# Moving the identity expert's eight wide operations from VectorE to GpSimd in an RWKV + mixture-of-experts layer

## The reference, cut to what matters

```python
x = x + rwkv(layernorm(x))                     # time-mix attention, not touched here
hid = layernorm(x)
probs = softmax(hid @ router_w + router_bias)  # 16 experts
top_w, top_i = top_k(probs, 2)
combine = one_hot(top_i, 16) * normed(top_w)   # zero for all but two experts of a token
routed = combine[:, 15:16] * hid               # expert 15 is the identity
for e in range(15):
    y = silu(hid @ gate_w[e]) * (hid @ up_w[e]) @ down_w[e]
    routed = routed + combine[:, e:e+1] * y
shared = silu(causal_conv3(hid)) * (hid @ shared_up_w) @ shared_down_w
out = x + shared + routed
```

## Time and profile before

| | us |
|---|---|
| median of 3 runs | 2799.32 (2798.11 to 2801.17) |
| the profiled execution's own time | 2799.06 |
| its span, on the slowest core (core 6) | 2797.3 |
| spans of the eight cores | 2783.8 to 2797.3 |
| busy on core 6: TensorE matmuls | 1857.6 |
| busy on core 6: VectorE | 1234.5 |
| busy on core 6: ScalarE | 364.3 |
| busy on core 6: GpSimd | 67.9 |

### The profile page before, as it was taken

The page is one execution under the profiler, slowest core; times in us unless marked ns, Lnnn a source line. Parts: engine busy times, 40 slices in busy tenths (PEclk is TensorE's granted clock), DMA queues, the critical chain, the costliest instruction groups (busy, mean ns, idle before and its releaser), DMA issues.

```text
span 2797.3 us, 21491 instructions; the slowest of 8 cores (2783.8 to 2797.3 us)
## 1 busy us (share of the span) xinstructions
PE 1857.6 (66%) x7497; PEld 784.3 (28%) x7648; DVE 1234.5 (44%) x1708; ACT 364.3 (13%) x615; POOL 67.9 (2%) x88
## 2 busy tenths in 40 slices
PE   3524336134043698788887887888878878888787
PEld 1201112011011243333333333333333333333333
DVE  4483583662666612344243343442433434434244
ACT  0411420323200000100100001001010010010100
POOL 0000000000010000000000000000000000000000
PEclk8756658577565799899998988989989989889898
DMA  7603305114062100212132132121321311213102
GB/s 151 120 1 60 60 0 90 30 21 70 0 91 45 25 0 1 35 18 38 18 51 38 16 53 34 20 38 16 53 38 16 53 21 32 38 16 53 31 0 120
DMA packets 69306, 112.77 MB, mean 40 GB/s; under 512 B 2592, under 2 KB 37424, under 8 KB 68160
## 3 DMA queue, kind: packets, MB, share of 16 engines
q0 software_dynamic: 63856, 94.50, 22.1%
q1 hardware_dynamic: 5344, 16.91, 1.7%
HBM read 197.28 MB, written 8.52 MB: 74 GB/s over the span
## 4 chain that ended last, share of the span: by engine, by line
PE 53%; DVE 10%; issue 2%; ACT 1%; DVEq 0%; DMA 0%; ACTq 0%; POOLq 0%
PE pc L704 18%; PE pc L730 16%; PE pc L718 15%; DVE h L773 4%; DVE sg L772 4%; PE pc L669 2%; PE pc L688 1%; ACT sg L802 1%; PE pc L677 1%; DVE acc L746 1%; DVE h L743 1%; DVE acc L781 1%; DVE h L755 0%; DVEq L36 0%; DMA cb<-comb_dram 0%
## 5 line engine op out<-in xcount | busy, mean ns | idle before, releaser
L704 PE MATMUL pc<-ln2x,wsl 128*128 128x512 bf16 x1882 | 511.5, 435 | 194.8 <-ACT sg L802 190.5
L730 PE MATMUL pc<-h,wsl 128*128 128x512 bf16 x1882 | 458.8, 404 | 104.4 <-DVE h L773 100.3
L772 DVE TENSOR_TENSOR sg<-sg,pc 128x512 f32<-128x512 f32 x240 | 165.0, 687 | 817.3 <-PE pc L718 798.3
L718 PE MATMUL pc<-ln2x,wsl 128*128 128x512 bf16 x1881 | 425.1, 380 | 2.1
L781 DVE TENSOR_TENSOR acc<-acc,pc 128x512 f32<-128x512 f32 x480 | 330.0, 688 | 184.5 <-PE pc L730 145.0
L704 PEld LDWEIGHTS pc<-ln2x,wsl 128*128 128x128 bf16 x1920 | 205.2, 109 | 500.0 <-issue 336.8
L802 ACT ACTIVATE sg<-pc 128x512 f32<-128x512 f32 x240 | 143.3, 597 | 1519.3 <-PE pc L704 1012.5
L730 PEld LDWEIGHTS pc<-h,wsl 128*128 128x128 bf16 x1920 | 190.2, 102 | 373.1 <-issue 192.8
L718 PEld LDWEIGHTS pc<-ln2x,wsl 128*128 128x128 bf16 x1920 | 187.6, 98 | 230.2
L371 PE MATMUL pb<-mx,wsla 128*128 128x512 bf16 x501 | 128.6, 421 | 180.4 <-DVE mx L225 156.9
L371 PE MATMUL pb<-sry,wsla 128*128 128x512 bf16 x251 | 65.0, 424 | 189.9 <-DVE sry L277 94.9
(11 more groups left out here) (121 smaller groups left out, 913.8 us busy)
## 6 DMA issues: line engine op xcount, KB each, us to landing
wsl<-gw POOLq DMA_DIRECT2D x15, 1024.0 KB, 9.5
wsl<-uw POOLq DMA_DIRECT2D x15, 1024.0 KB, 10.3
wsl<-dw POOLq DMA_DIRECT2D x15, 1024.0 KB, 10.4
acc<-x SPq DMA_DIRECT2D x4, 2048.0 KB, 24.9
wsla<-wk POOLq DMA_DIRECT2D x4, 2048.0 KB, 16.9
wsla<-wv POOLq DMA_DIRECT2D x4, 2048.0 KB, 18.4
wsla<-wr POOLq DMA_DIRECT2D x4, 2048.0 KB, 28.2
wsla<-wo POOLq DMA_DIRECT2D x4, 2048.0 KB, 16.9
```

Source lines behind the costliest of these rows:

```text
L704: inst = t.matmul(pc4[tc][:], slot_ap(3 * e)[:, kc, ocI * 128:(ocI + 1) * 128], ln2x[:, kc, 2 + tc * 512: 2 + (tc + 1) * 512], start=(kc = ...
L718: inst = t.matmul(pc4[4 + tc][:], slot_ap(3 * e + 1)[:, kc, ocI * 128:(ocI + 1) * 128], ln2x[:, kc, 2 + tc * 512: 2 + (tc + 1) * 512], sta ...
L730: inst = t.matmul(pc4[(oc % 2) * 4 + tc][:], slot_ap(3 * e + 2)[:, kcI, oc * 128:(oc + 1) * 128], h[:, kcI, tc * 512:(tc + 1) * 512], star ...
L772: VS.do(lambda sl=sl, tc=tc: v.tensor_tensor(sl[:], sl[:], pc4[4 + tc][:], OP.mult))
```

## The change

The eight operations of the identity expert leave VectorE's list and stand, with the same operands and the same order, at the head of GpSimd's list in `blk4`. GpSimd issues the DMA for row 15, waits for it itself, does the eight operations one behind the other, and only then issues the DMAs for rows 0 and 1; the wait for `v:id3` ahead of row 1 falls away, since GpSimd is now itself the reader of `cb[1]`. VectorE's list in the block begins with a wait for `g:id3`, the last of the eight, ahead of the first `hsh`.

```diff
-                gp_seq = ["comb15", "comb0", "comb1"]
+                gp_seq = ["comb0", "comb1"]
...
                 @blk4.gpsimd
                 def _(g):
+                    GS.eng = g
+                    g.dma_start(fl(cb[1][:]),
+                                comb_d[15][None, :].broadcast_to([128, T])).then_inc(s_cb[1], 16)
+                    g.wait_ge(s_cb[1], 16)
+                    for tc in range(4):
+                        cbc = cb[1][:, tc, :].unsqueeze(1).broadcast_to([128, CC, 512])
+                        hf = fl(h[:]).bitcast(F32).rearrange("p (cc t) -> p cc t", t=512)
+                        GS.do(lambda tc=tc, cbc=cbc, hf=hf: g.tensor_tensor(
+                            hf[:], ln2x[:, :, 2 + tc * 512: 2 + (tc + 1) * 512], cbc, OP.mult))
+                        dst = acc[:, :, tc * 512:(tc + 1) * 512] if "id" in parts else hf[:]
+                        GS.do(lambda tc=tc, dst=dst, hf=hf: g.tensor_tensor(
+                            dst, acc[:, :, tc * 512:(tc + 1) * 512], hf[:], OP.add), f"id{tc}")
...
                             if nm == "comb1":
-                                g.wait_ge(s_dv, MS("v:id3"))
+                                pass
...
                 @blk4.vector
                 def _(v):
                     VS.eng = v
-                    v.wait_ge(s_cb[1], 16)
-                    for tc in range(4):
-                        cbc = cb[1][:, tc, :].unsqueeze(1).broadcast_to([128, CC, 512])
-                        hf = fl(h[:]).bitcast(F32).rearrange("p (cc t) -> p cc t", t=512)
-                        VS.do(lambda tc=tc, cbc=cbc, hf=hf: v.tensor_tensor(
-                            hf[:], ln2x[:, :, 2 + tc * 512: 2 + (tc + 1) * 512], cbc, OP.mult))
-                        dst = acc[:, :, tc * 512:(tc + 1) * 512] if "id" in parts else hf[:]
-                        VS.do(lambda tc=tc, dst=dst, hf=hf: v.tensor_tensor(
-                            dst, acc[:, :, tc * 512:(tc + 1) * 512], hf[:], OP.add), f"id{tc}")
+                    v.wait_ge(s_gp, MS("g:id3"))
```

## The result

The changed kernel takes 2823.94 us (median of 10 runs) beside 2799.19 us of the kernel before on the same chips: the ratio is 1.0087, with a 95% interval of 1.0075 to 1.0099, thus 24.4 us more (21 to 28). The forecast was 2836, that is 37 us more, with 2815 to 2872 as its range.

What follows compares the result with a forecast made beforehand. The identity expert, ending last ahead of the first hsh, was taken to bound the block's start. 8 x 8.85 + 8 x 0.3 - 36.24 = +37.0 us on 2799.06 gave 2836 us, range 2815 to 2872.

Steps and rivals of the forecast that it cites:

- What bounds the place: Start of the feed-forward block: the identity expert ends 12.5 us after the up projection, so any lengthening is paid in full.
- The price of the eight operations: Identity expert on GpSimd: 8.85 us an operation, twice VectorE's 4.425, with ends of 2.29 and 15.5 us.
- The gaps: Between GpSimd's eight operations: 0.3 us each, taken between 0.11 and 0.53, 2.4 us in all.
- TensorE's clock after the longer wait: Ahead of the shared down projection: idle time grows from 15.86 to about 53 us; nothing added, 1.3 us either side.
- Costed at nothing with their cover: DMAs of rows 0 and 1 go out at about 1004; row 0 is first read at 1119.64, so no cost.
- What is after it follows rigidly: Behind the first hsh: four chunks and 15 experts shift with the delay, their length unchanged.
- Three passes: Rival on GpSimd's price: two reads and the write take turns, 13.3 us an operation, 2871 us; chance of 11.0 to 13.3 us 0.14.
- A load at first use: Rival ahead of GpSimd's first tensor operation: a load of 1.3 us, 2837, or about 6 us, 2842; chance 0.10.
- Faster: Rival: GpSimd at the bf16 product's 2.29 us an operation, hsh 12.4 us sooner, 2787 us; chance 0.03.
- no change: Rival: GpSimd at VectorE's own rate, +1.6 us, 2801; holds between 3.5 and 4.9 us an operation; chance 0.03.

Runs made afterwards that it cites:

- probe: The changed kernel with twelve more operations and two memsets on GpSimd while it waits for the first expert; 2825.4 us in one run.
- gp_apart: The changed kernel with a separate scratch tile for GpSimd's product, so no wait ahead of the first hsh; median 2789.9 us, ratio 0.9921.
- pad_ve: The changed kernel with eight memsets of 8 columns on VectorE ahead of its wait for g:id3; 2835.4 us in one run.

## Why the prediction was right, and where its sum was off

- **What bounds the place.** Right, to the tenth of a microsecond. The identity expert ended last and was paid in full: the wait of TensorE ahead of the down projection grew from 15.86 to 45.66 us, and leaving the work out won 12.4 us, the amount that was read from the rows.
- **The price of the eight operations.** The mis-sized term. It was put at 8 x 8.85 = 70.8 us, two passes of VectorE's time each. The additions fit, at 8.81; the products took 7.31, since their two bf16 inputs, one of them broadcast, are cheaper on GpSimd than two f32 ones (in `probe` and `gp_apart`, for 2048 elements: 4.51 us for f32, 4.05 for bf16, 3.75 for bf16 with the broadcast), while VectorE takes 4.425 us for both the earlier trace rows. Measured: 4 x 8.81 + 4 x 7.31 = 64.5 us. Two passes was a choice; `probe` supports it in so far as one input costs about half of two. The figure of the Trainium skill, "GPSIMD Engine Reference", section 3.1, agrees for f32: its 4497 ns for 2048 elements stand beside the 4.51 us of `gp_apart`'s additions. For the bf16 pair that table has no figure, and the prediction's 9.0 us would have been 1.7 us too much.
- **The gaps.** Put at 2.4 us, they were 1.3 us: 0.15 us between two of GpSimd's operations (937.20 to 937.35) and 0.31 us from the last to `hsh`. The 0.53 us of the row used as upper bound was the way to a DMA, not to an operation.
- **So far the sum** would have been 64.46 + 1.32 - 36.24 = +29.5 us instead of +37.0.
- **TensorE's clock after the longer wait.** Nothing added, within 1.3 us; right: the first down projection took 8.55 us after 45.66 us of idle time, beside 9.79 before, so the threefold idle time made nothing slower. But the 9.79 us were not the price of idling that the prediction read in them: `gp_apart`'s first down projection took 9.78 us after only 3.40 us of idle time.
- **Costed at nothing with their cover.** Right: the DMAs of rows 0 and 1 go out at 995.31, and nobody waits for them.
- **"What is after it follows rigidly."** This step was wrong by 6 us. The part behind the first `hsh` became 1825.0 instead of 1831.3 us (means of eight cores), 5.0 us less between the two slowest ones. Four steps are 6.9 us shorter, and `pad_ve` shows what makes them so: the removal of eight operations from VectorE's list moved its breaks. Ahead of the fourth step and in the last expert the differences go either way, and what sets them is open. The prediction counted what these operations cost while they run, not that the list is shorter. Together: +29.5 - 5.0 is +24.5, and the two profiled cores began 1.1 us apart, which gives the +23.4 us between their spans; the runs show +24.4. The three errors, in the price, the gaps and the rest, all made the forecast too high, by 12 us together, half of the measured change; the range held because it was drawn for prices from 6.2 to 13.3 us.
- **The rivals.** Three passes: no operation came near 13 us. A load at first use: the first product took 7.30 us like the others and started 5.6 us after its DMA's issue, beside 5.4 before, so no 1.3 us and no 6 us. The Trainium skill, "GPSIMD Engine Reference", section 2.1, states about 6 us for the first call to a freshly loaded kernel; the trace shows nothing of the kind ahead of this operation. Faster and no change: both needed an operation under 4.9 us.

Left open: what a break is. That VectorE's list is loaded in pieces fits the traces: 940 of the 960 breaks are followed within 4.5 us by a packet of 8192 bytes in the profile's instruction queue. Behind the break at 1815.3 us of the kernel before (core 6) it is the only transfer from 1815 to 1817 us:

```profile
DMA packets 1, 0.01 MB, mean 4 GB/s; under 512 B 0, under 2 KB 0, under 8 KB 0
...
q14 instruction: 1, 0.01, 1.5%
```

The packet starts after the break, and whether the loading is its cause no run shows. Open too is by what way the places of the breaks act on the granted clock (0.83 or 0.91) and the length of the matmuls behind them.

## What to carry to other kernels

Before moving work to a slower engine, ask whether its result is waited for where it stands: if the waiting operation doesn't need the values but only the memory, a tile of its own is the change to make, and then either engine will do (13.7 and 13.3 us less here). An operation with two inputs on GpSimd cost 1.7 to 2.2 ns an element, twice what VectorE took at the upper end, and a copy about 1.0 ns, so that a move pays only under cover. And expect the time of a kernel of this kind to move by some 5 to 9 us, here 0.2 to 0.3%, when the number of instructions in VectorE's list changes: compare the parts that weren't edited before a small difference is put down to an edit.

## What the runs showed of the hardware that was not expected

- VectorE leaves 0.46 us instead of 0.11 us between operations at every 128th instruction of its list, waits included (960 of 960 such places in twelve kernels), where it isn't waiting or busy anyway; eight idle memsets of 0.07 us and their waits moved these places, and the untouched part grew from 1825.0 to 1834.2 us, 6.9 us of it in four experts.
- Stretches with the same work, 64 matmuls each, last 19.96 us at a granted clock of 0.91 and 20.6 us at 0.83. The lengths of the experts that come of it are the same on all cores of a kernel to 0.05 us from the sixth on and go with the places of these breaks.
- GpSimd took 3.60 us for an operation on one f32 tile used as both inputs, 2048 wide, and 4.51 us on two different ones.
- GpSimd's additions (4.51 us) and VectorE's `dash` (0.69 us) took as long beside each other as alone.
